# Cross-attention block: softmax weights split query-major and transposed by DMA instead of by TensorE

## What is computed

```python
q, kv = ln(x), ln(ctx)
qp, kp, vp = q @ Wq.T + bq, kv @ Wk.T + bk, kv @ Wv.T + bv
scores = einsum('bhld,bhtd->bhlt', qh, kh) / sqrt(32)
scores = scores - spatial_scale[h] * dist(q_xy, t_xy) + spatial_offset[h]   # masked keys -inf
attn_out = einsum('bhlt,bhtd->bhld', softmax(scores), vh)
x = x + attn_out @ Wo.T + bo
out = x + gelu(ln(x) @ W1.T + b1) @ W2.T + b2
```

## Time and profile before

| | us |
|---|---|
| median of 2 runs | 1420.86 (1420.81 to 1420.9) |
| the profiled execution: its time | 1420.8 |
| the profiled execution: its span | 1419.0 |
| busy in the span: TensorE matmul / VectorE / ScalarE / POOL | 1381.1 / 859.4 / 811.9 / 706.7 |
| DMA moved, queue q1 | 118.35 MB, 30.3% of 16 engines' span |

### The profile page before, as it was taken

One profiled execution on the slowest core, in us unless ns is written; L12 is line 12 of the kernel. 1 busy time (PEld: TensorE's weight loads), 2 busy tenths in 40 slices (PEclk: granted clock), 3 DMA queues, 4 the chain that ended last, 5 costly groups with the idle time before them and its releaser, 6 DMA issues.

```text
span 1419.0 us, 25885 instructions
## 1 busy us (share of the span) xinstructions
PE 1381.1 (97%) x8860; PEld 1166.1 (82%) x8860; DVE 859.4 (61%) x2557; ACT 811.9 (57%) x2003; POOL 706.7 (50%) x1049
## 2 busy tenths in 40 slices
PE   6899999999999999999899999999999999999999
PEld 2589888898888889888688888888888888888887
DVE  6599999999999999989835322232222322223211
ACT  4599989898989999998734323222222222222221
POOL 2588888889888888899621201212012120121200
PEclk9899999999999999999999999999999999999999
DMA  4545555565555556455421100101001010010000
GB/s 172 135 101 126 137 147 144 141 156 134 147 131 130 141 138 157 126 145 147 160 104 38 60 1 0 60 1 60 1 1 60 1 60 1 0 60 0 31 1 30
DMA packets 67076, 120.01 MB, mean 85 GB/s; under 512 B 9088, under 2 KB 9344, under 8 KB 66944
## 3 DMA queue, kind: packets, MB, share of 16 engines
q1 hardware_dynamic: 66944, 118.35, 30.3%
HBM read 50.94 MB, written 16.78 MB: 48 GB/s over the span
## 4 chain that ended last, share of the span: by engine, by line
PE 62%; DVE 16%; POOL 7%; issue 6%; ACT 5%; DMA 2%; SPq 1%; DVEq 0%; ACTq 0%; POOLq 0%
PE ps_s L571 12%; PE ps_qk L557 12%; PE ps_pt L571 12%; PE ps_tr L557 12%; DVE pT L839 4%; PE ps_qk L490 4%; DVE soft L829 3%; POOL soft L1121 3%; POOL soft L1129 2%; PE ps_pt L453 2%; PE ps_vo L516 2%; PE ps_vo L513 2%; DVE qk_parts L845 1%; ACT soft L657 1%; DVE stats L877 1%
## 5 line engine op out<-in xcount | busy, mean ns | idle before, releaser
L978 DVE TENSOR_TENSOR hid<-gelu,hid 128x512 fp32r<-128x512 f32 x128 | 94.7, 740 | 509.7 <-ACT hid L747 509.7
L1121 POOL TENSOR_SCALAR soft<-soft,row_stats 128x256 f32<-128x256 f32 x512 | 246.6, 495 | 58.8 <-DVE row_stats L835 58.2
L657 ACT ACTIVATE soft<-soft,row_stats 128x256 f32<-128x256 f32 x512 | 255.5, 507 | 0.3
L490 PE MATMUL ps_qk<-xT,w_qkv_sb 128*128 128x256 f32 x1536 | 230.8, 293 | 3.3 <-DVE qk_parts L845 3.2
L490 PEld LDWEIGHTS ps_qk<-xT,w_qkv_sb 128*128 128x128 f32 x1536 | 196.9, 192 | 4.3 <-DVE qk_parts L845 4.1
L571 PE MATMUL ps_s<-w,hid 128*128 128x512 f32 x768 | 199.2, 395 | 0.0
L1129 POOL TENSOR_SCALAR soft<-dist,scale_neg,offset 128x512 f32<-128x512 f32 x256 | 197.1, 770 | 0.2 <-ACT dist L681 0.2
L571 PE MATMUL ps_pt<-w,hid 128*128 128x512 f32 x768 | 195.3, 390 | 0.0
L829 DVE CUSTOM_DVE_ANT_0 soft<-ps_s,soft 128x256 f32<-128x256 f32 x512 | 193.0, 413 | 3.8 <-POOL soft L1129 2.0
L557 PE MATMUL ps_qk<-hT,w 128*128 128x512 f32 x768 | 184.8, 389 | 0.9 <-ACT gelu L744 0.9
L557 PE MATMUL ps_tr<-hT,w 128*128 128x512 f32 x768 | 184.6, 389 | 0.0
(11 more groups left out here) (97 smaller groups left out, 2012.7 us busy)
## 6 DMA issues: line engine op xcount, KB each, us to landing
stack<-qk_parts SPq DMA_DIRECT2D x256, 192.0 KB
raw<-in_ctx SPq DMA_DIRECT2D x32, 256.0 KB, 3.2
raw<-in_x SPq DMA_DIRECT2D x32, 256.0 KB, 3.1
x_t<-in_x SPq DMA_DIRECT2D x32, 256.0 KB, 2.6
x_scratch<-x_t SPq DMA_DIRECT2D x32, 256.0 KB, 2.7
x_g<-x_scratch SPq DMA_DIRECT2D x32, 256.0 KB, 3.4
w_raw<-in_w SPq DMA_DIRECT2D x8, 1024.0 KB, 8.0
out<-x_g SPq DMA_DIRECT2D x32, 256.0 KB, 2.2
```

The costliest lines, as they stand in the source:

```text
L490: mm = e.matmul(ps_qk[:, which * L:(which + 1) * L], w_qkv_sb[:, wp, k, col:col + P], xT[:, b % 2, which, xp, k, :], start=(k, wp, xp) == ...
L657: e.activation(soft[:, ring, lc, :], soft[:, ring, lc, :], ACT.Exp, scale=-1.0, bias=neg_max[:, ring, lc:lc + 1], accum_out=row_sum[:, rin ...
L978: e.tensor_tensor(hid[s % 3][:, LO, :], gelu[:, s % 2, :], hid[s % 3][:, HI, :].bitcast(F32), ALU.subtract).then_inc(s_hlo)
L1121: e.tensor_scalar(soft[:, ring, lc, :], soft[:, ring, lc, :], row_inv[:, ring, lc:lc + 1], P_SCALE, ALU.mult, ALU.mult).then_inc(s_norm)
```

## The change

The weights are split before they are transposed. `normalise` writes the normalised weights once as fp16, query-major, into a new ring `p_nat` of two items (the high part; the factor 2^14 is now put into the inverse by an additional VectorE `tensor_scalar` of 128x2 that waits for the reciprocal). `p_lo` moves to slot i+4, before it was i+5, and becomes two `scalar_tensor_tensor` of 128x256: `soft` times the inverse minus the high part, all operands in SBUF. Then SP issues one transposing DMA of 128x1024 fp16 (256 KB) from `p_nat` to `pT`, first in SP's slot i+4. `normalise(i)` waits until the DMA of item i-2 has landed. TensorE's four transposes and ScalarE's `p_hi` are gone; `attend` and the three steps after it come one slot later. `soft` has 6 tiles instead of 7, and a tile is free after `p_lo`. `b_2` moves in SBUF, and the first three MLP steps' `mlp_gelu` and `hid_lo` move from slots N+2 and N+3 to N+4 (N = 256), `mlp_up(2)` from N+3 to N+4.

```diff
-        SOFT_RING, PT_RING, STACK_RING, DIST_RING = 7, 6, 3, 4
+        SOFT_RING, NAT_RING, PT_RING, STACK_RING, DIST_RING = 6, 2, 6, 3, 4
+        p_nat = sb("p_nat", [P, NAT_RING, 2, LC, T], F16)
-        pT = sb("pT", [P, PT_RING, 2, TC * L], F16)
+        pT = sb("pT", [P, PT_RING, 2 * LC * TC, P], F16)
@@ sync_program
+            def p_transpose(i):
+                gate.wait_ge(s_plo, 2 * i + 2)
+                gate.wait_ge(s_brow, N_BROW[SEC_V])
+                if i >= PT_RING:
+                    gate.wait_ge(s_pv, (i - PT_RING) // 4 + 1)
+                e.dma_start_transpose(pT[:, i % PT_RING, :, :], p_nat[:, i % NAT_RING, :, :, :].rearrange("p w c t -> p (w c t)")).then_inc(s_pt[i % PT_RING], DMA)
...
+                    for i in due(slot, 4, ITEM, N_ITEMS):
+                        p_transpose(i)
@@ tensor_program
-            def p_transpose(i):
-                gate.wait_ge(s_norm, 2 * i + 2)
-                gate.wait_ge(s_ptlo, i - 1)
-                for tc in range(TC):
-                    for lc in range(LC):
-                        tr = e.transpose(ps_pt[i % 2][:, tc * L + lc * P:tc * L + (lc + 1) * P],
-                                         soft[:, i % SOFT_RING, lc, tc * P:(tc + 1) * P], ident[:])
-                tr.then_inc(s_t)
@@ attend
-                gate.wait_ge(s_ptlo, 4 * G + 4)
+                for i in range(4 * G, 4 * G + HPG):
+                    gate.wait_ge(s_pt[i % PT_RING], n_pt(i))
@@ scalar_program
-            def p_hi(i):
-                gate.wait_ge(s_t, i + 1)
-                if i >= PT_RING:
-                    gate.wait_ge(s_pv, (i - PT_RING) // 4 + 1)
-                e.activation(pT[:, i % PT_RING, 0, :], ps_pt[i % 2][:], ACT.Copy).then_inc(s_pthi)
@@ vector_program
             def inverse(i):
                 gate.wait_ge(s_exp, 2 * i + 2)
-                gate.wait_ge(s_norm, 2 * (i - SOFT_RING) + 2)
-                e.reciprocal(row_inv[:, i % SOFT_RING, :], row_sum[:, i % SOFT_RING, :]).then_inc(s_inv)
+                gate.wait_ge(s_plo, 2 * (i - SOFT_RING) + 2)
+                inv = row_inv[:, i % SOFT_RING, :]
+                e.reciprocal(inv, row_sum[:, i % SOFT_RING, :]).then_inc(s_inv)
+                gate.wait_ge(s_inv, 2 * i + 1)
+                e.tensor_scalar(inv, inv, P_SCALE, None, ALU.mult).then_inc(s_inv)
 
             def p_lo(i):
-                gate.wait_ge(s_pthi, i + 1)
-                e.tensor_tensor(pT[:, i % PT_RING, 1, :], ps_pt[i % 2][:], pT[:, i % PT_RING, 0, :], ALU.subtract).then_inc(s_ptlo)
+                ring, nat = i % SOFT_RING, i % NAT_RING
+                for lc in range(LC):
+                    gate.wait_ge(s_norm, 2 * i + lc + 1)
+                    e.scalar_tensor_tensor(out=p_nat[:, nat, LO, lc, :], in0=soft[:, ring, lc, :], scalar=row_inv[:, ring, lc:lc + 1],
+                                           in1=p_nat[:, nat, HI, lc, :], op0=ALU.mult, op1=ALU.subtract).then_inc(s_plo)
@@ gpsimd_program
             def normalise(i):
                 ring = i % SOFT_RING
-                gate.wait_ge(s_inv, i + 1)
+                gate.wait_ge(s_inv, 2 * i + 2)
+                if i >= NAT_RING:
+                    gate.wait_ge(s_pt[(i - NAT_RING) % PT_RING], n_pt(i - NAT_RING))
                 for lc in range(LC):
-                    e.tensor_scalar(soft[:, ring, lc, :], soft[:, ring, lc, :], row_inv[:, ring, lc:lc + 1], P_SCALE,
+                    e.tensor_scalar(p_nat[:, i % NAT_RING, HI, lc, :], soft[:, ring, lc, :], row_inv[:, ring, lc:lc + 1], 1.0,
                                     ALU.mult, ALU.mult).then_inc(s_norm)
```

More of the change, by code:

```diff
@@ L129, in build_block @@
         v_norm = sb("v_norm", [P, D], F32, at["pT"] + KT * D * 4)
+        v_scale = sb("v_scale", [P, D], F32, at["pT"] + (KT + 1) * D * 4)
         bias_w = sb("bias_w", [P, 3 * KT], F32)
@@ L146, in build_block @@
         x1_n = sb("x1_n", [P, 2, D], F32, at["tok_rows"])
-        b_2_sb = sb("b_2", [P, D], F32, at["x1_g1"] + GT * D * 4)
+        b_2_sb = sb("b_2", [P, D], F32, at["mask_row"])
         hid_bytes = 2 * GROUP_TOK * 4
@@ L151, in build_block @@
         gelu = sb("gelu", [P, 2, GROUP_TOK], F32, at["qk_parts"] + hid_bytes)
-        assert at["w_1_0"] + CHUNKS * chunk_bytes + 2 * KT * GROUP_TOK * 4 <= at["raw"] and at["b_2"] + D * 4 <= at["attnT"]
+        assert at["w_1_0"] + CHUNKS * chunk_bytes + 2 * KT * GROUP_TOK * 4 <= at["raw"] and at["x1_g1"] + GT * D * 4 <= at["attnT"]
         assert at["w_2_0"] + chunk_bytes <= at["qk_parts"] and at["gelu"] + 2 * GROUP_TOK * 4 <= at["soft"]
@@ L190, in build_block @@
         s_bias, s_score, s_max, s_exp, s_inv, s_norm = [sem(n) for n in ("s_bias", "s_score", "s_max", "s_exp", "s_inv", "s_norm")]
-        s_t, s_pthi, s_ptlo, s_pv, s_y, s_ahi, s_alo = [sem(n) for n in ("s_t", "s_pthi", "s_ptlo", "s_pv", "s_y", "s_ahi", "s_alo")]
+        s_plo, s_pt, s_pv, s_y, s_ahi, s_alo = sem("s_plo"), sems("s_pt", PT_RING), sem("s_pv"), sem("s_y"), sem("s_ahi"), sem("s_alo")
         s_o, s_res, s_x1, s_x1st = sem("s_o"), sem("s_res"), sem("s_x1"), sem("s_x1st")
@@ L220, in n_stack, with n_pt @@
             return 5 * DMA * (G // STACK_RING + 1)
+        def n_pt(i):
+            return DMA * (i // PT_RING + 1)
         N_W_LO = {SEC_K: KT, SEC_Q: 2 * KT, SEC_V: KT, SEC_O: 2 * KT}
@@ L565, in mlp_down @@
                 gate.wait_ge(s_max, 2 * N_ITEMS)
-                gate.wait_ge(s_ptlo, N_ITEMS)
                 for i in range(GT):
@@ L581, in tensor_program @@
                         scores(i)
-                    for i in due(slot, 4, ITEM, N_ITEMS):
-                        p_transpose(i)
-                    for G in due(slot, 9, GROUP, N_HG):
+                    for G in due(slot, 10, GROUP, N_HG):
                         attend(G)
@@ L603, in tensor_program @@
                         mlp_up(slot - N_ITEMS + 2)
-                    if slot == N_ITEMS + 3:
+                    if slot == N_ITEMS + 4:
                         mlp_up(2)
@@ L742, in mlp_gelu @@
                 gate.wait_ge(s_score, N_ITEMS)
+                for i in range(N_ITEMS - NAT_RING, N_ITEMS):
+                    gate.wait_ge(s_pt[i % PT_RING], n_pt(i))
                 gate.wait_ge(s_stack[(N_HG - 1) % STACK_RING], n_stack(N_HG - 1))
@@ L750, in scalar_program @@
                 if slot < LAST_SLOT:
-                    for i in due(slot, 5, ITEM, N_ITEMS):
-                        p_hi(i)
                     for G in due(slot, -7, GROUP, N_HG):
@@ L763, in scalar_program @@
                         exps(i)
-                    for G in due(slot, 12, GROUP, N_HG):
+                    for G in due(slot, 13, GROUP, N_HG):
                         attn_hi(G)
@@ L797, in scalar_program @@
                         w2_hi(m)
-                    if slot == N_ITEMS + 2:
+                    if slot == N_ITEMS + 4:
                         mlp_gelu(0)
                         mlp_gelu(1)
-                    if slot == N_ITEMS + 3:
                         mlp_gelu(2)
@@ L1010, in vector_program @@
                             x_lo(b, i)
-                    for G in due(slot, 11, GROUP, N_HG):
+                    for G in due(slot, 12, GROUP, N_HG):
                         attn_scale(G)
@@ L1188, in gpsimd_program @@
                         bias_tile(i)
-                    for G in due(slot, 13, GROUP, N_HG):
+                    for G in due(slot, 14, GROUP, N_HG):
                         attn_lo(G)
```

9 lines of the change are left out of this document (4 added, 5 removed).

## The result

The changed kernel takes 1875.18 us (1871.38 to 1878.97, 2 runs) where the kernel before takes 1420.86: a ratio of 1.3198, 95% interval 1.3083 to 1.3312. That is 454 us more; the prediction said 339 more (1760, range 1530 to 2050).

A forecast was written before the change was run, and what follows sets the result against it. VectorE was taken to bound the kernel before, TensorE nearly equal. 256 slots x (3.78 - 2.47) = 335, + 4 for one later slot = 339 us on 1420.8: 1760 us, range 1530 to 2050 (8 in 10).

The forecast's parts named there:

- the first case: Attention: a loop through DMA and POOL, lengthened by SP, sets 3.78 us a slot, 1760 us; chance 0.48.
- VectorE bounds the kernel before: Attention, kernel before: VectorE is the bound with 2.45 us of work per 2.47 us slot, TensorE equal within a hundredth.
- The loop through DMA, `normalise`, bias and `score_max`: Attention, two `p_nat` tiles: from `p_lo` round to `p_lo` two items later, 7.31 us for two slots, 3.66 per slot.
- The landing: Transposing DMA, issue to landing: 3.2 us, priced by a 256 KB load; 2.6 to 4.2 us as bounds.
- SP's queue: SP, once in four slots: transposition, `qk_lo` wait and stack copies (3.57 us) delay the next transposition; 3.78 us per slot.
- VectorE's additions: VectorE per slot: subtractions +0.29 net, waits +0.38, scaling +0.25, making 3.37 us from 2.45.
- The wait for POOL's operations: VectorE's two subtractions with both inputs in SBUF: each waits 0 to 0.38 us for POOL, taken as 0.19.
- DMA engines: The 16 DMA engines: 1.36 us per slot plus 1.03 for the transposition, 2.4 of 3.78, no bound.
- the fourth rival: TensorE in attention: its clock falls to 1.2 GHz, its work becomes 4.04 us and the bound, 1827 us; chance 0.07.
- the third rival: Transposing DMA is slow: landing 8.0 us gives 2341 us, 5 us gives 1960, eight serial blocks some 2660; chance 0.20.
- The signs: Profile after: POOL waits for the DMA, VectorE for POOL's bias; slot 3.6 to 3.9 us; MLP half unchanged.
- the second case: Attention: VectorE alone bounds, its own 2.84 to 3.37 us per slot; at 3.1, 1586 us; chance 0.20.

The follow-up runs named there:

- b_scale: The kernel before with only the additional 128x2 scaling of the inverse on VectorE, its factor taken out of POOL's scaling: 1482.0 us, ratio 1.0422.
- three tiles: The changed kernel with three `p_nat` tiles instead of two, five `pT` tiles instead of six, and `attend` back in its earlier slot: 1678.5 us.
- the exchange: The changed kernel with `bias_tile` put before `normalise` in POOL's slot: 1733.2 us, ratio 1.2196.
- actq: The changed kernel with its transposing DMAs issued by ScalarE, in its slot i+5, instead of SP: 1894.6 us.

## Why the prediction was right, and where it was short

The measured 1875 lies in the range of 1530 to 2050, and the mechanism of the first case is the one that the runs show. The range is wide, and the sum was 115 us short: 3.78 us a slot forecast, 4.21 measured.

- *VectorE bounds the kernel before*: shown by b_scale. The forecast that freeing TensorE and ScalarE gives nothing by itself follows from it; no run frees them alone.
- *The loop through DMA, `normalise`, bias and `score_max`*: the waits name it link by link, and three tiles and the exchange each shorten it. Forecast 7.31 us for two slots, measured 7.13.
- *The landing*, 3.2 by a plain load: 3.1 median. In part this was luck. The plain copy within SBUF lands in 2.4, so the transposition costs 0.7 more than a copy, and the row it was priced by happened to stand as high.
- *SP's queue*: the term that was too small. The forecast had 11.75 us from the `p_lo` before the copies to the third one after it, and 3.37 for the fourth slot, 15.1 together. On the timeline the first is 496.75 to 509.36, 12.61: 2.36 in place of 2.12 to the copies, because the DMA's own issue stands before them (1.35, `qk_lo` runs beside it); 3.69 in place of 3.57 for the copies; 3.66 in place of 3.2 from the delayed issue to `normalise`; and 2.90 in place of 2.86 from there. The fourth slot costs half an undisturbed trip, 3.5 to 3.6, and not VectorE's 3.37, because each of the two tiles closes a loop of its own. So four slots take a trip of 7.1 and one of 9.0, 16.1.
- *The rest to the measured 16.8.* A term at nothing: the store and reload of the residual, for which SP waits once in 16 slots. The transposition of 520.01 was issued only at 523.48, and the step after the long one took 4.59 in place of 3.5 (525.49 to 530.08); those four slots, 516.48 to 533.38, took 16.9, the four before them 16.1. Averaged over all that is 0.2. The other 0.5 are steps beside the copies longer than those of the example (long ones 5.7 in the mean, not 5.48); their causes I did not measure apart.
- *VectorE's additions*: two subtractions 0.87, measured 0.87. The wait for POOL's operations, put at 0.19 each, was 541 - 477 (median) = 0.06 here and 569 - 477 = 0.09 with POOL busier; the scaling 0.205, not 0.25. VectorE's own slot is 2.94, not 3.37. This term was too large and hid part of the SP term that was too small. The single waits are still there (`p_lo`'s longest operation is 1.58 us), but they are rarer than the 0.92 us of line 882 made them look: the same scaling, now line 883, takes 0.53 here with POOL at 54%.
- *DMA engines*: 1.03 us forecast per transposition at the rate of plain transfers, 1.54 to 1.66 measured. No bound at 4.21 us a slot; 2.9 us of work in each, which comes near once the loop is opened.
- *The clock* fell, as the fourth rival said, to 0.64 to 0.80 in attention, and TensorE's matmuls got longer (a 128x256 of `attend` 421 ns in the median, 273 before). Its 1827 us is nearer to the measured time than the 1760 of the sum, but the mechanism is not its: it has TensorE full, and TensorE has 260.44 / 95 = 2.74 us of work in a slot of 4.21.
- *The slow transposition* of the third rival did not come: 3.1 us for eight blocks of 128x128 together, so a price of 1309 ns for each, one after another, is no way to count them. That transposing DMAs are as fast as regular ones (the Trainium skill, Advanced Engine Details and Errata, "X-Bar Transpose (TRN2)") does not hold here either: 1.54 against 0.72 us of the engines, 3.1 against 2.4 us to landing.
- *The signs* named for it: the waits, the landing, ScalarE's 45% and the MLP half came as said. The slot of 3.6 to 3.9, TensorE at 45 to 55% (65%, at the lower clock) and the pair of subtractions at 1.1 to 1.5 us (1.08) did not.
- *Sums that do not come out of their terms*: 1690 to 1890 by the waits' bounds is 1692 to 1820 at a landing of 3.2, and 1654 to 1916 with the landing's bounds as well; the 3.19 of the second case also needs the scaling at its lower 0.10. The main sum is not touched.

## What to carry to other kernels

Before work is moved off an engine, ask which engine sets the slot; here the freed ones were not it, and the full one got two elements more per partition for 59 us. When a DMA replaces an on-chip step between engines, write down the whole circle from the release of the buffer to its next use, with everything that stands behind the waiting instruction in each in-order queue, divide by the number of buffers, and do so for each buffer's own circle. Then the cheapest cure can be the order, here 142 us for two operations exchanged: what does not need the DMA goes ahead of what waits for it.

## What the runs showed of the hardware

- A transposing DMA of 128x1024 fp16 within SBUF: 1.23 us to issue, 3.0 to 3.1 us from issue to landing undisturbed, and 1.54 us of the 16 DMA engines by difference (1.66 by its own queue's row in actq), in 1056 packets; the plain copy 0.48, 2.4 and 0.72, in 144.
- Issued on ScalarE's queue while SP issues copies (actq, at 492.77), it took 2.17 us instead of 1.25, and POOL went on 5.95 us after the issue began; a load on SP behind them took 2.25 us instead of 0.58 (medians of `raw<-in_ctx` 1.60 and 0.58). A second queue did not make the two independent.
- A VectorE operation on two elements per partition is not free: the scaling of 128x2 takes 0.17 us in the median and 0.21 (kernel after) to 0.29 (b_scale) in the mean, and lengthened the slot of a kernel that VectorE bounds by 0.23 (b_scale).
